# Third edge pass of a four-layer graph network: messages summed by node with one-hot products into PSUM blocks, in place of a turned scan and end gathers

## The reference

```python
# layer 0, twice: msg = x[src] @ W_msg + ea32 @ W_edge ; agg = segment_max(msg, dst)
# layer 1:
h = relu(ea17 @ W1.T + b1); w = h @ W2.T + b2
msg = w * x[src]
agg = segment_sum(msg, dst, N)                 # 96 features per node
x = layernorm(x + relu(x @ Ws.T + bs + agg @ Wn.T + bn))
# layer 2: two hops of a degree-normalised sum over the edges
# layer 3: one such sum, then a product with a weight
```

## Time and profile before

| | us |
|---|---|
| median of 3 runs (4448.87 to 4472.46) | 4451.47 |
| span of the profiled execution | 5118.6 |
| gathers of pass 0, first to last | 1220.1 |
| gathers of pass 1 | 1205.8 |
| gathers of pass 2 | 1326.2 |
| all else (5118.6 less these three) | 1366.5 |

### The profile page before, as it was taken

One profiled execution on the slowest core, in us unless ns is written; L12 is line 12 of the kernel. 1 busy time (PEld: TensorE's weight loads), 2 busy tenths in 40 slices (PEclk: granted clock), 3 DMA queues, 4 the chain that ended last, 5 costly groups with the idle time before them and its releaser, 6 DMA issues.

```text
span 5118.6 us, 56111 instructions
## 1 busy us (share of the span) xinstructions
PE 4044.6 (79%) x19316; PEld 2656.8 (52%) x19316; DVE 2232.8 (44%) x5877; ACT 1002.8 (20%) x2108; POOL 2581.0 (50%) x2689
## 2 busy tenths in 40 slices
PE   5777767677368776777764998998898969999999
PEld 4333333333333333333333655555555649999999
DVE  3454555555124444444443555555555552222211
ACT  1100000000122222222223333333333330001101
POOL 4666666665556666666655665566566530000000
PEclk9999999999965667666655566556666559999999
DMA  5333333333234444444432443434343327777776
GB/s 136 100 99 89 102 95 100 89 101 88 48 93 136 124 135 127 137 121 138 131 100 66 117 122 114 123 115 123 110 127 108 117 84 268 269 266 268 263 260 219
DMA packets 251432, 695.04 MB, mean 136 GB/s; under 512 B 80458, under 2 KB 163082, under 8 KB 219914
## 3 DMA queue, kind: packets, MB, share of 16 engines
q1 hardware_dynamic: 56126, 348.35, 21.2%
q0 software_dynamic: 85568, 131.83, 12.0%
q10 hardware_dynamic: 109516, 212.06, 11.4%
HBM read 477.94 MB, written 214.09 MB: 135 GB/s over the span
## 4 chain that ended last, share of the span: by engine, by line
PE 59%; another core or an unknown queue 14%; DVE 12%; issue 10%; ACT 2%; DMA 1%; POOL 1%; DVEq 0%; ACTq 0%; POOLq 0%; SPq 0%
PE banks L1118 17%; PE banks L981 9%; PE banks L1022 7%; PE banks L976 6%; PE banks L956 6%; PE banks L947 5%; PE banks L995 5%; DVE scan L1831 5%; DVE hot_lo L1483 3%; DVE hot_hi L1485 1%; PE banks L735 1%; DVE hot_key L1848 1%; DVE hot_src L1850 1%; ACT adj L1350 1%
## 5 line engine op out<-in xcount | busy, mean ns | idle before, releaser
L709 POOL DMA_INDIRECT gath<-table,ids x2496 | 2406.3, 964 | 1425.4 <-issue 698.5
L1831 DVE TENSOR_TENSOR_SCAN scan<-keep_of,scan,banks 96x512 f32<-96x512 bf16 x621 | 791.3, 1274 | 1737.9 <-remote 972.9
L1118 PE MATMUL banks<-r_parts,adj_in 128*128 128x288 bf16 x7203 | 890.2, 286 | 5.1 <-DVE r_parts L1531 2.6
L1118 PEld LDWEIGHTS banks<-r_parts,adj_in 128*128 128x128 bf16 x7203 | 883.2, 142 | 7.4 <-DVE r_parts L1531 3.4
L995 PEld LDWEIGHTS banks<-ident,scan 96*128 96x128 f32 x2496 | 400.9, 224 | 911.7 <-issue 505.7
L995 PE MATMUL banks<-ident,scan 96*128 96x96 f32 x2496 | 528.4, 359 | 325.7 <-DVE scan L1831 254.5
L981 PE MATMUL banks<-ea_of,w_edge_of 32*96 32x512 f32 x832 | 765.1, 1016 | 0.3 <-issue 0.3
L1022 PE MATMUL banks<-hot_key,hot_src 128*128 128x392 bf16 x1600 | 543.3, 475 | 272.8 <-issue 139.3
L1332 ACT ACTIVATE back<-banks 128x384 f32<-128x384 f32 x624 | 305.2, 489 | 2062.0 <-remote 873.4
L1848 DVE TENSOR_SCALAR hot_key<-iota_key,key_t 128x392 bf16<-128x392 int16 x1600 | 505.4, 316 | 21.0 <-ACT key_t L1371 21.0
L956 PEld LDWEIGHTS banks<-w_edge_out,hid 97*128 97x128 f32 x1664 | 320.2, 287 | 307.2 <-issue 305.4
(11 more groups left out here) (158 smaller groups left out, 2100.9 us busy)
## 6 DMA issues: line engine op xcount, KB each, us to landing
adj_in<-adjacency SPq DMA_DIRECT2D x147, 1568.0 KB
scanned_rows<-back ACTq DMA_DIRECT2D x153, 768.0 KB
adjacency<-adj ACTq DMA_DIRECT2D x100, 784.0 KB
gath<-table,ids POOLq DMA_INDIRECT x2496
ea_of<-in_ea_t SPq DMA_DIRECT2D x78, 512.0 KB
keep_of<-keep_max_d SPq DMA_DIRECT2D x52, 768.0 KB
keep_of<-keep_sum_d SPq DMA_DIRECT2D x26, 768.0 KB
table<-x_sb SPq DMA_DIRECT2D x10, 240.0 KB, 4.4
```

The costliest lines, as they stand in the source:

```text
L709: pool.indirect_dma_start(gath[:, b, t, :], None, tables[p][:, :], bass.IndirectOffsetOnAxis(ap=ids[:, 1, n:n + 1], axis=0),).then_inc(s_g ...
L1118: m = pe.matmul(sum_ps[:, u, j, :], adj_in[:, a, :, h], r_parts[:, n % 2, h, :, :].rearrange("p k f -> p (k f)"), start=h == 0, stop=h == ...
L1831: ve.tensor_tensor_scan(scan[0:D, b, at:at + Q], keep_of[:, i % 2, CHUNK * b + at:CHUNK * b + at + Q], turn_ps[k % 2], start, keep_op, tak ...
```

## The change

Pass 2 no longer turns, scans, turns back, stores rows, or fetches ends. A node block is 128 nodes, and there are 50; on average a block takes 17 edge tiles (`PER`). A tile is multiplied into the block that its place names and, within 6 tiles of a border (`MARGIN`), into the neighbour too, from a one-hot of its targets that is 256 places wide. Two more terms in the choice of the branch test at the start that no target strays further than that. Sums of a block pile up in one PSUM bank (of two, in turn), and ACT copies each finished block to `agg_all`. `keep_of` is not loaded in pass 2, and POOL issues no end gathers there.

```diff
+PER = 17
+MARGIN = 6
+SPAN = 2 * P
+def base_of(tile):
+    return (tile + PER - MARGIN) // PER - 1
+def blocks_of(tile):
+    base, place = base_of(tile), tile % PER
+    both = (base,) if MARGIN <= place < PER - MARGIN else (base, base + 1)
+    return [h for h in both if h >= 0]
+def first_tile(h):
+    return max(0, PER * h - MARGIN)
+def last_tile(h):
+    return min(TILES, PER * (h + 1) + MARGIN) - 1
...
+                hot_dst = back[:, :, :].rearrange("p b x -> p (b x)")[:, 0:2 * QT * SPAN]\
+                    .rearrange("p (h t c) -> p h t c", h=2, t=QT)
...
+        seg_ps = [banks[:, b, 0:D] for b in (0, 1)]
+        wide_w_ps = [banks[:, b, 0:QT * D] for b in (4, 5)]
...
 # SP
+                        if KIND[p] == EDGE17:
+                            return
...
 # POOL
-                    nodes(p)
+                    if p < 2:
+                        nodes(p)
...
 # PE, pass 2
+                        def hidden(q):
+                            ...
+                            if q >= 2:
+                                pe.wait_ge(s_hid, q - 1)
+                            pe.matmul(hid_ps[q % 2], weights(2), columns, start=True, stop=True).then_inc(s_hid_ps, 1)
+                        def edge_rows(q):
+                            pe.wait_ge(s_hid, q + 1)
+                            if q >= 2:
+                                pe.wait_ge(s_msg, q - 1)
+                            for t in range(QT):
+                                m = pe.matmul(wide_w_ps[q % 2][:, t * D:(t + 1) * D], hid[:, q % 2, t * P:(t + 1) * P],
+                                              W["edge_out"][:, :], start=True, stop=True)
+                            m.then_inc(s_w, 1)
+                        def sum_quarter(q):
+                            pe.wait_ge(s_msg, q + 1)
+                            for t in range(QT):
+                                tile = QT * q + t
+                                for h in blocks_of(tile):
+                                    if tile == first_tile(h) and h >= 2:
+                                        pe.wait_ge(s_seg_out, h - 1)
+                                    c = P * (h - base_of(tile))
+                                    m = pe.matmul(seg_ps[h % 2], hot_dst[:, q % 2, t, c:c + P], msg_now[:, q % 2, t * D:(t + 1) * D],
+                                                  start=tile == first_tile(h), stop=tile == last_tile(h), skip_group_check=True)
+                            m.then_inc(s_seg, 1)
+                        ...
+                        for q in range(QUARTERS):
+                            if q + 3 < QUARTERS:
+                                hidden(q + 3)
+                            if 1 <= q <= 8 * BUILT:
+                                count_windows((q - 1) // 8, (q - 1) % 8)
+                            if q + 2 < QUARTERS:
+                                edge_rows(q + 2)
+                            sum_quarter(q)
...
 # ACT, pass 2
+                        def leave_sums(q):
+                            for h in ENDING[q]:
+                                act.wait_ge(s_seg, q + 1)
+                                act.activation(agg_all[:, h, :], seg_ps[h % 2], ACT.Copy).then_inc(s_seg_out, 1)
...
 # DVE, start of pass 1: 50 short instructions put each edge's target, less its block's first node, in flag
+                        for a in range(NT):
+                            tiles = slice(max(0, PER * a - (PER - MARGIN)), min(TILES, PER * a + MARGIN))
+                            ve.tensor_scalar(flag[:, tiles], ids[:, 0, tiles], float(-P * (a - 1)), None, ALU.add)
 # DVE, pass 2
+                        def hots_of_dst(q):
+                            if q >= 2:
+                                ve.wait_ge(s_seg, q - 1)
+                            ve.tensor_tensor(hot_dst[:, q % 2, :, :],
+                                             flag[:, QT * q:QT * (q + 1)].unsqueeze(2).to_broadcast([P, QT, SPAN]),
+                                             iota_b[:, :].unsqueeze(1).to_broadcast([P, QT, SPAN]), ALU.is_equal)
+                        ...
+                        for q in range(QUARTERS):
+                            if q + 1 < QUARTERS:
+                                hots_of_dst(q + 1)
+                                message(q + 1)
+                            if q < 8 * BUILT:
+                                window_hots(q // 8, q % 8)
```

More of the change, by code:

```diff
@@ L772, in turn_nodes @@
                 def turn_nodes(i, b, first):
-                    if p == 2:
+                    if p == 2 and not fast:
                         pe.wait_ge(s_agg[n][b], 16 * GT * (i + 1))
-                    else:
+                    elif p != 2:
                         pe.wait_ge(s_node[n], 2 * i + b + 1)
@@ L779, in turn_nodes @@
                     for t in range(GT):
[L780 to L781 removed]
+                        of_node = node[:, b, t, :] if p != 2 else agg_all[:, (2 * i + b) * GT + t, :] if fast else agg[:, b, t, :]
+                        m = pe.transpose(node_turn_ps[:, t * P:(t + 1) * P], of_node, ident[:, :])
                     m.then_inc(s_nturn[n], 1)
@@ L804, in nodes @@
                           5: [(turn_nodes, 0), (multiply_y, 0)]}.get(p)
-                if stages:
+                if fast and p == 2:
+                    pe.wait_ge(s_seg_out, NT)
+                    for g in range(GROUPS):
+                        for stage, _ in stages:
+                            stage(g // 2, g % 2, g < 2)
+                elif stages:
                     over_groups(pe, *stages)
@@ L1056, in _ @@
                     if KIND[p] == EDGE17:
-                        hidden(0, 0)
-                        hidden(0, 1)
-                        edge_rows(0, 0)
+                        sum_by_node()
+                        nodes(p, before_ps, fast=True)
+                        continue
                     def pair(i, first, last):
                         for k in range(8):
-                            if KIND[p] == EDGE17 and not (last and k > 5):
-                                hidden(i + (k + 2) // 8, (k + 2) % 8)
-                            if KIND[p] == EDGE17 and not (last and k == 7):
-                                edge_rows(i + (k + 1) // 8, (k + 1) % 8)
                             turn_back(i, k, first)
@@ L1447, in _ @@
             ve.memset(eps[:, :], EPS)
+            ve.memset(strays[:, :], 0.0)
             ve.memset(ends[:, NT:], 0)
@@ L1633, in nodes @@
                         ve.wait_ge(s_adj[half], 16 * 2 * BUILT)
-                over_groups(ve, (end_ix_ahead, 0), *{0: [(add_and_rectify, 0)],
+                over_groups(ve, *[(end_ix_ahead, 0)] * (not (dense and p == 2)), *{0: [(add_and_rectify, 0)],
                                   1: [(add_and_rectify, 0), (factors, 0)],
@@ L1873, in pair @@
                                 window_hots(i, k)
-                            if KIND[p] == EDGE17 and not (last and k == 7):
-                                message(i + (k + 1) // 8, (k + 1) % 8)
                             scan_quarter(i, k, first)
```

161 lines of the change are left out of this document (92 added, 69 removed).

## The result

The changed kernel takes 4578.1 us (median of 4 runs, 4529.8 to 4609.8), the kernel before 4450.2 (4 runs): ratio 1.0256, 95% interval 1.0208 to 1.0303. It is slower. (The ratios in this document are estimates with their intervals, and not quotients of the two medians; that would be 1.0287 here.) Six more runs of it, timed later beside 21 of the kernel before, gave 4575.1 against 4444.1 and the same ratio, 1.0256 (1.0202 to 1.0309). Its times scatter: 4530 to 4610, and that will matter. Runs more than 1.5% above the fastest of their kernel are slow ones and stay out of the ratios: one of the changed kernel (4609.8), three of `e4_none` and two of `e5_twice`, the profiled executions of these two among them.

A forecast was written before the change was run, and what follows sets the result against it. The prediction took POOL's gathers to bound all three passes. From 4451.5 us it added 54 for contention, took off 21 for end gathers and added 2 for the prologue: 4486, with a range of 4370 to 4720.

The forecast's parts named there:

- POOL's gathers bound pass 2 of the kernel before: All three passes, pass 2 too, were taken as bound by POOL issuing 832 gathers, about 1028 us a pass.
- faster: Rival: timed pass 2 is 120 us longer than pass 1 because PE is behind; that goes, giving 4312; chance 0.12.
- Contention, +54 (21 to 210): Pass 2: DVE's added target comparison, with both operands in SBUF, slows POOL's gathers by 54 us over 208 quarters.
- I take 0.26, near the mean row: Loss in us per quarter of pass 2 from DVE's comparison, chosen between bounds of 0.10 and 1.01.
- The rule weighed: Skill page on DVE against POOL: its inference would make the pass 2 term 0, its first rule 250 us.
- Row path removed, 0: Pass 2 loses turns, scans, copies, row stores and `keep_of` loads; none is ahead of a gather, so 0 us.
- Sums on PE: Pass 2: 6.8 added products a quarter make PE's quarter 8.14 us low, 4.31 high; more high-clock time expected, counted 0.
- PE becomes the bound at the low clock: Rival: in pass 2 PE falls behind at its low level, 239 us more, 4671, or 5085 if always low; chance 0.18.
- End gathers, -21: After the last message and in the node stage, removing end gathers saves 12 and 9 us.
- Prologue, +2: Two DMAs and a few short DVE instructions ahead of the branch choice delay the first gather, 0 to 4 us.
- no contention: Rival: DVE's long comparison in pass 2 falls between POOL's readings and costs nothing, giving 4432; chance 0.22.
- full contention: Rival: DVE's comparison costs POOL 1.01 us per quarter of pass 2, 210 us, giving 4642; chance 0.08.

The follow-up runs named there:

- e4_none: The changed kernel without the 1024-place comparisons after the first two quarters of pass 2, so sums come out wrong: 4444.0 us, ratio 1.0011.
- e5_twice: The changed kernel with the whole 1024-place comparison made twice in a row, a drain between: 4615.5 us, ratio 1.0366.
- e10_again: The changed kernel, unchanged, run again for more times and a second profile: 4534 to 4591 us, the profiled run 4589.9.
- e7_order: The changed kernel with PE's counting products moved from ahead of the edge weights to just ahead of the sums: 4517.8 us, ratio 1.0159.
- e1_psum: The changed kernel with each quarter's targets first copied to PSUM, so the comparison has only one SBUF operand: 4494.7 us, ratio 1.0137.
- e6_before_plus: The kernel before with one unused 1024-place comparison of two SBUF operands added ahead of each message of pass 2: 4537.0 us, ratio 1.0201.

## Why the prediction was right, and where it was off

- **POOL's gathers bound pass 2 of the kernel before.** Right: 4.9 us of waits for the message in 1065. The way to it was wrong. I laid 1366.5 us of "all else" on the timed run and got 1.236 us per gather. Undisturbed, the passes are 1.27 to 1.28 per gather and all else is 4452.6 - 3187.2 = 1265.4; the 1366.5 of the disturbed execution was 101 too long, and so the pace came out too short. That a wrong "all else" still gave the right bound was luck. The premise of the rival "faster", 120 us of pass 2 over pass 1, is gone too: they are equal (1065.1 and 1065.5).
- **Contention, +54 (21 to 210).** The right mechanism, and the term that was mis-sized: the gathers of pass 2 are 100 us longer than before, and the comparison added alone cost 96. The step that failed is "I take 0.26, near the mean row". That row gave 0.10, and nothing leads from it to 0.26. It is also the wrong row: its mean of 985 ns comes from 50 gathers with pauses between them, where only 3 of the 20 sums of 0.66 us had a gather start in their first 0.4 us. Those three took 1.42, 1.22 and 1.16. The one of 1.42 held the rule: it ended 0.81 after DVE. From it: a gather that starts x after DVE is held to its end, unless x is past about 1.1 of 1.22; with a gather each 1.25 us, at a chance x, that is on average 1.09 x 1.09 / 2 / 1.25 = 0.475 us per comparison, 99 us. Measured 100 / 208 = 0.48 (0.45 when added alone).
- **The rule weighed.** The Trainium skill's page "SBUF — State Buffer", section "Who interferes with whom", speaks of this case. By its first rule, two SBUF inputs of VectorE against GpSimd's reads, the trace agrees (1096 with, 959 without the second one). Its inference that descriptor generation is spared is not borne out for these indirect gathers, which also read their indices `ids`.
- **Row path removed, 0.** Right for the waits: ACT's busy time fell from 409 to 319 us and DMA's share from 0.51 to 0.30, and POOL's idle time stayed (266 and 270). But without the comparison a gather takes 958 ns (`e4_none`), where the kernel before has 976: (976 - 958) x 832 = 15 us less. So the comparison itself costs (1096 - 958) x 832 = 115 us in the changed kernel, and the 100 are what is left of it. Which of the parts removed gives the 15 no run shows.
- **Sums on PE.** The prices held: 0.225 us per half at the low level, and 7.58 for a quarter of 12 halves; with the mean of 2 x 6.8 = 13.6 halves that is 7.58 + 1.6 x 0.225 = 7.94 (8.14 forecast). What failed is "I expect more time at the high level than before, and count 0". The clock of pass 2 was 0.76 before and 0.75 after, so products in place of turns did not raise it. In `e10_again` PE fell behind for rows of quarters, and by the mean clocks so it did in most timed runs, which is argued and not shown. The price at the median is 131 - 72 = about 60 us, by `e7_order`. This is the rival "PE becomes the bound at the low clock", at a quarter of its price of 239. I had priced it against POOL at 5.0 us a quarter. The contention had slowed POOL to 5.6, so PE needs (8.14 - 5.6) / (8.14 - 4.31) = 0.66 of the quarters at the high level instead of 0.82. The two costs cover each other: taking contention away (`e1_psum`) brought 74 us, the order alone 59, both together 131 + 42 = 173, which is 40 more than the two apart.
- **End gathers, -21.** Measured -21.1, 11.6 and 9.5 for the forecast 12 and 9. A further 11 went because PE had no backlog at the end of this pass, which I hadn't counted. **Prologue, +2:** measured 2.3.
- **The sum.** By the first profile of the changed kernel it is 101.5 - 32.4 + 2.3 = 71 us. `e7_order`, whose pass 2 is as long, is near that: 4517.8 - 4445.8 = 72. About 60 of PE's low stretches on top give +131, as timed. Forecast +34.5. The time of 4578 lies in the range of 4370 to 4720 and on the side forecast; of the sum, one term was half its size and one was counted at nothing.
- The rivals "no contention" and "full contention" are out by `e6_before_plus`; the rival "faster" was out from the start, as above.

Left open: why the clock keeps to its low level in some executions of the same program and not in others, why another order of the same products raises it, and what disturbed the first profiled execution.

## What to carry to other kernels

When POOL issues indirect gathers back to back, expect a long DVE instruction with two tensor operands in SBUF to cost up to about its own length per instruction (here 1.08 of 1.22 us at most, 0.48 on average), and more than in proportion to its length. Put one operand in PSUM, or try a form with a per-partition scalar. Both are shown for this one kernel. Size such a term from the single worst row and the chance of meeting it, not from a mean over a stretch with another rhythm. And a term that slows the bounding engine gives the next one slack: before removing it, ask who is second (here PE, at its low clock), and look at several executions if times scatter.

## What the runs showed of the hardware

- A gather that is held ends 0.81 to 0.83 us after the end of DVE's instruction, whether it had started 0.03, 0.15 or 0.43 into it. One that was 0.82 us old when DVE's began kept its 0.94.
- Comparisons of one piece, two, and four back to back gave gathers of 1096, 1004 and 1023 ns on average; a gather could be held over four pieces, 2.22 us.
- The same products of PE per quarter gave a granted clock over pass 2 of 0.77 with the bf16 counting products between the `ea_of` product (32 rows) and the edge weights (97 rows), and of 0.90 with them next to the sums (128 rows). The time went from 4495 to 4403 us, and the scatter of its runs from 42 (4 runs) to 7 us (6 runs).
- Beside a chain of scalar comparisons without a pause a gather took up to 2.00 us, nine of 832 over 1.2.
